# Tiles normalised and turned ahead of the seam: four in the token experts, six in cross attention with four tiles' gate logits

## The chip, the cores and the metric

One NeuronCore of a Trainium2 chip runs the whole kernel. Its engines are TensorE (matmuls and transposes into PSUM), VectorE, ScalarE, GpSimd and SyncE, which here only issues DMAs; each works through a queue of its own, and they wait for one another by semaphores. The metric is the time of one execution in microseconds (us), as the median of several; less is better.

## The reference, cut to what matters

A decoder of two layers on 1024 tokens of width 256, everything in float32 at the edges. Every step reads a layer norm of the running `x` and adds to it:

```python
x = x + linear_attention(layernorm(x))     # L0: 16 heads, decaying sums
x = x + token_experts(layernorm(x), ids)   # L0: 4 experts chosen by token id
x = x + retrieval(layernorm(x))            # L0: 2025 products of keys, top 8 of 8 heads
x = x + block_attention(layernorm(x))      # L1
x = x + cross_attention(layernorm(x), ctx) # L1: 16 heads of 16, quantised
h = layernorm(x)                           # L1: router
scores = sigmoid(h @ gate_w.T)
_, topk_idx = top_k(scores + bias, 2)      # of 16 experts
x = x + shared(h) + routed(h, topk_idx, scores)
```

The layer norm is `(x - mean) / sqrt(var + eps)` per token, without gain or offset.

## The kernel before

`x` lies in SBUF as 8 tiles (`NT`) of 128 tokens by 256. `xT` is the normalised and transposed state, 2 chunks (`DC`) of 128 by 1024 tokens. Each stage is a `Block`: within it every engine has its own list of instructions, and the next block begins when all engines have come to the end of theirs. This document calls that point a seam.

The layer norm is spread over seam and engines. In the tail of a stage, VectorE adds the result of a tile to `x` and takes its statistics (`norm_statistics`, L90); behind the eighth tile it writes the variances to `ln.rstd` (L104) and GpSimd raises them to the power -0.5 (`norm_pool`, L118). Behind the seam, VectorE normalises eight tiles (`norm_vector`, L111), TensorE turns each with two transposes (`norm_tensor`, L135, two PSUM banks in turn) and ScalarE copies each to `xT` (`norm_scalar`, L143). TensorE spends the wait at the end of a stage on products of the identity whose result nobody reads (`keep_busy`, L124; four calls are eight instructions in the trace).

The order of the work is written out by hand. At the first seam (A) `token_experts` ends with a product per tile (L479) and `private_state` begins. Its up products (L572, 8 groups of 4 instructions) read only the first 512 tokens of `xT`, the tiles 0 to 3. TensorE waits for the keys (L609) and for all eight copies (L610) before them. ScalarE follows each group with a silu (L632), and behind the last ones with casts (L1444) which VectorE's `quantise_context` (L1447 to L1480) needs.

At the second seam (B) `attend`, the core of cross attention, ends. It runs 128 units (8 tiles of 16 heads): scores on TensorE (L1761), their maximum and a bias on VectorE (L1822, L1824), the exponential on ScalarE (L1811), a cast on GpSimd (L1748), a DMA transpose that SyncE issues (L1733), and eight units later the mix with the values on TensorE (L1771). For each tile there follows a finish: `normalise` (L1834), two transposes (L1780), `scale_values` (L1846), the projection (L1786, L1787), and `residual` (L1851) with the statistics. For the tiles 0 to 6 it is done inside the loop over the next tile's units, for tile 7 it is the tail. Then `route` normalises and turns eight tiles, makes the gate's logits (L1999, 32 instructions), their sigmoid (L2019), and VectorE's selection (from L2033 on): the picks (L2048), from which TensorE counts ranks (L2006, L2009), and the slots (to L2073). `mix_experts` follows, the expert stage.

## Time and profile before

| | |
|---|---|
| median of 3 runs | 977.1 us (976.2 to 977.96) |
| profiled execution | 974.31 us, of which the span from first to last instruction is 972.3 |
| busy share of the span | TensorE 79%, VectorE 75%, GpSimd 58%, ScalarE 58% |
| mean granted TensorE clock | 0.894 of full speed |
| seam A | at about 137 us of the span |
| cross attention's units | from about 636 to 836 us |
| seam B | at about 847 us |

In the traces below PE is TensorE's matmuls, PEld its weight loads, DVE VectorE, ACT ScalarE, POOL GpSimd, SPq SyncE's queue; `out<-in` are the names of the program, and `x8` says that eight instructions were merged into one line whose length is theirs together. In brackets stands how long the engine was idle before, and what ended the wait. The time of an execution lies some 2 us above its span.

### The profile page before, as it was taken

The page shows a single profiled execution, that of the slowest core. Times are in us where ns is not written, and L with a number is a line of the kernel's source. Part 1 is how long each engine was busy: PE and PEld are TensorE (multiplying, and loading weights), DVE is VectorE, ACT ScalarE, POOL GpSimd, SP SyncE. Part 2 cuts the span into 40 slices and gives each one's busy share as a digit, 9 for nine tenths or more (in the row PEclk, how much of TensorE's full clock was granted, in tenths as well). Part 3 has the DMA queues.
Part 4 walks back from the last instruction along what each step waited for, and adds up shares of the span by engine and source line. Part 5 has one row for each costly group of instructions (what it writes and reads, how often), then busy time and mean ns, then how long its engine had stood idle before and what let it go on. Part 6 is the DMA issues. An engine that isn't in the chain of part 4 may idle for free. (4 is left out here: it accounts for less than half of the span.)

```text
span 972.3 us, 14012 instructions
## 1 busy us (share of the span) xinstructions
PE 764.8 (79%) x4650; PEld 495.1 (51%) x4673; DVE 727.4 (75%) x1281; ACT 561.6 (58%) x1035; POOL 563.7 (58%) x440
## 2 busy tenths in 40 slices
PE   4999998868776777788879988766766767789991
PEld 2564663437665666666663466623333333356550
DVE  4766357688999999999942754679999999454564
ACT  2314114778678768777741454678888888224540
POOL 3115300799699998998931132258777776314642
PEclk9999999999999988978989989958777786799996
DMA  5002021000000000000006000969999999322224
GB/s 178 1 0 87 1 84 54 0 1 1 1 1 0 1 1 1 1 0 1 1 1 233 1 1 2 307 116 186 185 170 178 182 168 172 67 93 71 85 70 162
DMA packets 149525, 69.61 MB, mean 72 GB/s; under 512 B 139003, under 2 KB 144909, under 8 KB 148302
## 3 DMA queue, kind: packets, MB, share of 16 engines
q1 hardware_dynamic: 147150, 62.42, 29.3%
q0 software_dynamic: 2304, 6.29, 2.2%
q8 instruction: 38, 0.62, 0.3%
q14 instruction: 33, 0.27, 0.1%
HBM read 27.46 MB, written 7.68 MB: 36 GB/s over the span
## 5 line engine op out<-in xcount | busy, mean ns | idle before, releaser
L773 POOL TENSOR_TENSOR r_pairs<-r_side_exp 128x945 f32<-128x945 f32 x104 | 183.6, 1804 | 0.0
L902 ACT ACTIVATE r_w<-r_w,r_down 128x1024 f32<-128x1024 f32 (+1 forms) x119 | 134.8, 1136 | 63.7 <-DVE r_w L1004 53.0
L1811 ACT ACTIVATE c_probs<-c_scores,c_bias,c_q_scale 128x1024 int16<-128x1024 f32 x128 | 154.1, 1204 | 29.8 <-DVE c_bias L1824 20.9
L1748 POOL CAST kv_parts<-c_probs 128x1024 bf16<-128x1024 int16 x128 | 132.1, 1039 | 54.6 <-ACT c_probs L1811 53.3
L1822 DVE TENSOR_REDUCE c_neg_max<-c_scores 128x1 f32<-128x1024 f32 x128 | 155.5, 1215 | 6.1 <-PE c_scores L1761 5.9
L843 PE MATMUL r_head_sum<-ident,r_w 128*128 128x128 f32 x952 | 125.2, 291 | 36.4 <-ACT ctxT L913 21.8
L1761 PE MATMUL c_scores<-c_kT,c_placed 128*128 128x512 bf16 x233 | 98.6, 509 | 57.7 <-ACT c_probs L1811 54.3
L843 PEld LDWEIGHTS r_head_sum<-ident,r_w 128*128 128x128 f32 x952 | 116.2, 153 | 52.2 <-issue 34.3
L994 DVE SCALAR_TENSOR_TENSOR r_chosen<-r_pairs,r_kept,r_z 128x1024 f32<-128x1024 f32 (+1 forms) x84 | 103.5, 1272 | 4.5 <-ACT r_pairs L892 3.3
L1004 DVE TENSOR_TENSOR r_w<-r_pairs,r_chosen 128x1024 f32<-128x1024 f32 (+1 forms) x78 | 91.2, 1204 | 0.0
L803 PE MATMUL r_head_sum<-r_up,ctxT 128*128 128x256 f32 x224 | 61.3, 441 | 19.3 <-ACT ctxT L913 19.3
L1771 PEld LDWEIGHTS c_mixed<-c_v,c_pT 128*128 128x128 bf16 x1024 | 45.1, 103 | 46.8 <-issue 24.4
L803 PEld LDWEIGHTS r_head_sum<-r_up,ctxT 128*128 128x128 f32 x224 | 49.7, 225 | 29.5 <-ACT ctxT L913 20.8
L118 POOL TENSOR_TENSOR ln_rstd<-ln_rstd,ln_minus_half 128x8 f32<-128x8 f32 x6 | 9.9, 1650 | 88.2 <-DVE ln_rstd L104 86.3
L1761 PEld LDWEIGHTS c_scores<-c_kT,c_placed 128*128 128x128 bf16 x256 | 16.8, 105 | 81.4 <-ACT c_probs L1811 75.6
L892 ACT ACTIVATE r_pairs<-r_side_exp 128x45 f32<-128x45 f32 x208 | 56.3, 320 | 0.0
L1771 PE MATMUL c_mixed<-c_v,c_pT 128*128 128x32 bf16 x1024 | 45.5, 183 | 5.3 <-DMA c_pT<-kv_parts 5.1
L1091 POOL TENSOR_TENSOR b_p<-b_p,b_row_sum 128x1024 f32<-128x1024 f32 x8 | 15.2, 1896 | 58.7 <-DVE b_row_sum L1085 58.7
L755 POOL TENSOR_TENSOR r_w<-r_pairs,r_w 128x1001 f32<-128x1001 f32 x18 | 38.9, 2162 | 16.1 <-DVE r_w L994 16.1
L794 PE MATMUL r_z<-r_down,r_hT 128*128 128x512 f32 (+1 forms) x64 | 33.4, 647 | 12.6 <-DVE r_chosen L994 12.4
L773 POOL TENSOR_TENSOR r_late_pairs<-r_side_exp 128x945 f32<-128x945 f32 x24 | 42.7, 1803 | 0.0
L2132 POOL DMA_INDIRECT pick_rows<-e_made,e_to_row x24 | 23.8, 990 | 29.6 <-DVE e_made L2307 24.5
(354 smaller groups left out, 1607.0 us busy)
## 6 DMA issues: line engine op xcount, KB each, us to landing
en_w<-in_w SPq DMA_DIRECT2D x1, 2992.0 KB, 12.1
ew_w<-in_w SPq DMA_DIRECT2D x1, 2992.0 KB, 12.1
ew_w_near<-in_w_near SPq DMA_DIRECT2D x1, 2176.0 KB, 20.9
r_up<-in_up SPq DMA_DIRECT2D x1, 2048.0 KB, 9.6
c_pT<-kv_parts SPq DMA_TRANSPOSE x128, 3.3
token_rows<-e_xn SPq DMA_DIRECT2D x2, 1024.0 KB, 5.8
e_row<-pick_rows SPq DMA_DIRECT2D x8, 256.0 KB, 4.6
zero_rows<-b_zeros SPq DMA_DIRECT2D x1, 1360.0 KB, 14.9
```

What stands on the lines that cost most here:

```text
L773: nc.gpsimd.tensor_tensor(pair_slot(v)[:, BY_ACT * KEYS:].rearrange("p (a b) -> p a b", b=KEYS), a.broadcast_to([P, ROWS - BY_ACT, KEYS]), ...
L803: last = nc.tensor.matmul(to, wT[0:n, b, :], r.up[0:n, b, :], start=(b == 0), stop=(b == PB - 1))
L843: last = nc.tensor.matmul(head_sum[0:m, b // 4, (b % 4) * P:(b % 4 + 1) * P], w_slot(v)[:, b * P:b * P + m], ident[:, :], start=(h == 0 an ...
L892: last = nc.scalar.activation(pair_slot(v)[:, a * KEYS:(a + 1) * KEYS], side_exp[:, t % 2, HEADS_R + h, 0:KEYS], ACT.Copy, scale=side_exp[ ...
L902: nc.scalar.activation(w_slot(v)[:, 0:COLS[f]], w_slot(v)[:, 0:COLS[f]], ACT.Silu, scale=scale[:, t % 2, h:h + 1]).then_inc(silu_done, 1)
L994: nc.vector.scalar_tensor_tensor(to, products(v), kept[:, t % 2, h, TOP - 1:TOP], flat(z[:, :, :], f), ALU.is_ge, ALU.mult).then_inc(picke ...
L1004: nc.vector.tensor_tensor(w_slot(v)[:, 0:COLS[f]], products(v), flat(chosen[:, (v - pool_count(v)) % 2, :, :], f), ALU.mult).then_inc(weig ...
L1748: nc.gpsimd.tensor_copy(rounded[:, u % ROUNDED, :], probs[:, u % RING, :]).then_inc(rounded_ready, 1)
L1761: last = nc.tensor.matmul(scores[:, u % SCORED, n, :], placed[:, t % 2, h // 2, h % 2, :], s.kT[:, h // 2, n * HALF:(n + 1) * HALF], start ...
L1771: last = nc.tensor.matmul(mixed[:, 0, h * PAIR_C:(h + 1) * PAIR_C], pT[:, u % TURNED, n, :], s.v[:, n, h // 2 * PAIR_C:(h // 2 + 1) * PAIR ...
L1811: nc.scalar.activation(probs[:, u % RING, :], scores[:, u % SCORED, :, :].rearrange("p a b -> p (a b)"), ACT.Exp, bias=bias[:, t, h:h + 1] ...
L1822: chain.step(nc.vector.tensor_reduce(neg_max[:, t, h:h + 1], scores[:, u % SCORED, :, :].rearrange("p a b -> p (a b)"), AX.X, ALU.max, neg ...
```

## The change

Four things. (1) `norm_statistics` and `norm_pool` can do the norm in two parts, and the loops over tiles are split into functions for one tile. (2) In `token_experts` the tiles 0 to 3 are normalised (while the tiles 5 and 6 are being added), turned and copied before the seam; `private_state` normalises and turns the tiles 4 to 7, and TensorE does so behind the first group of up products, with the wait for the keys moved to the last group and a wait for the earlier loads put first, on SyncE too. (3) In `attend` the statistics of the tiles 0 to 5 are closed at tile 5 and raised to the power behind the cast of unit 117. VectorE normalises these six after the residual of tile 6, TensorE turns four of them between the last mixes and two behind the last projection, into banks of the scores, and makes four tiles' gate logits, two of them ahead of the last projection; ScalarE copies and takes their sigmoid. The gate is loaded at the start of `attend`. `route` does the rest: tiles 6 and 7, and the logits of the tiles 4 to 7. The normalised rows lie in `ctxT`, over which the expert stage writes, so VectorE waits there until they are stored. (4) The identity products go from 4 calls to 2 at the end of the token experts, from 4 to none at the end of `attend`, and from 4 to 2 ahead of the ranks.

The diff, cut to its core:

```diff
...
-def norm_statistics(nc, eng, sh, t):
+def norm_statistics(nc, eng, sh, t, first=NT):
...
     ln = sh.ln
     nc.vector.bn_stats(ln.stats[:, t, :], sh.x[:, t, :]).then_inc(ln.steps, 1)
-    if t >= 1:
+    if t >= 1 and t != first:
         nc.vector.bn_aggr(ln.mv[:, t - 1, :], ln.stats[:, t - 1, :]).then_inc(ln.steps, 1)
         ln.step_count += 1
     ln.step_count += 1
     eng.wait_ge(ln.steps, ln.step_count)
-    if t == NT - 1:
+    if t in (first - 1, NT - 1):
+        part = slice(0 if t == first - 1 else first, t + 1)
         nc.vector.bn_aggr(ln.mv[:, t, :], ln.stats[:, t, :]).then_inc(ln.steps, 1)
         ln.step_count += 1
         eng.wait_ge(ln.steps, ln.step_count)
-        nc.vector.tensor_scalar(ln.rstd[:, :], ln.mv[:, :, 1], LN_EPS, None, ALU.add).then_inc(ln.var_ready, 1)
+        nc.vector.tensor_scalar(ln.rstd[:, part], ln.mv[:, part, 1], LN_EPS, None, ALU.add).then_inc(ln.var_ready, 1)
 def norm_vector(nc, eng, ln, x, chain):
-    eng.wait_ge(ln.rstd_ready, ln.norms + 1)
-    for t in range(NT):
+    eng.wait_ge(ln.rstd_ready, ln.norms + 1 + ln.extra)
+    norm_rows(nc, ln, x, range(NT))
+def norm_rows(nc, ln, x, tiles):
+    for t in tiles:
         nc.vector.tensor_scalar(ln.xn[:, t, :], x[:, t, :], ln.mv[:, t, 0:1], ln.rstd[:, t:t + 1],
                                 ALU.subtract, ALU.mult).then_inc(ln.normed, 1)
...
-def norm_pool(nc, pool, ln, norm):
...
-    pool.wait_ge(ln.var_ready, norm + 1)
-    nc.gpsimd.tensor_tensor(ln.rstd[:, :], ln.rstd[:, :], ln.minus_half[:, :], ALU.pow).then_inc(ln.rstd_ready, 1)
+def norm_pool(nc, pool, ln, norm, part=slice(0, NT)):
+    pool.wait_ge(ln.var_ready, norm + 1 + ln.extra)
+    nc.gpsimd.tensor_tensor(ln.rstd[:, part], ln.rstd[:, part], ln.minus_half[:, part], ALU.pow).then_inc(ln.rstd_ready, 1)
...
-        pe.wait_ge(ln.normed, ln.tiles + t + 1)
-        if t >= 2:
-            pe.wait_ge(ln.copied, ln.tiles + t - 1)
-        for c in range(DC):
...
-        last.then_inc(ln.turned_ready, 1)
+        norm_turn(nc, pe, ln, ident, ln.turned, ln.tiles, t)
+def norm_turn(nc, pe, ln, ident, turned, tiles, t):
+    pe.wait_ge(ln.normed, tiles + t + 1)
+    if t >= 2:
+        pe.wait_ge(ln.copied, tiles + t - 1)
+    for c in range(DC):
+        last = nc.tensor.transpose(turned[:, t % 2, c * P:(c + 1) * P], ln.xn[:, t, c * P:(c + 1) * P], ident[:, :])
+    last.then_inc(ln.turned_ready, 1)
...
     for t in range(NT):
-        act.wait_ge(ln.turned_ready, ln.tiles + t + 1)
-        nc.scalar.copy(place(t), ln.turned[:, t % 2, 0:D].rearrange("p (c n) -> p c n", c=DC)).then_inc(ln.copied, 1)
+        norm_copy(nc, act, ln, place(t), ln.turned, ln.tiles, t)
+def norm_copy(nc, act, ln, to, turned, tiles, t):
+    act.wait_ge(ln.turned_ready, tiles + t + 1)
+    nc.scalar.copy(to, turned[:, t % 2, 0:D].rearrange("p (c n) -> p c n", c=DC)).then_inc(ln.copied, 1)
...
+        FIRST = NT // 2
+        tiles = (ln.norms + 1) * NT
...
-            norm_pool(nc, pool, ln, ln.norms + 1)
+            norm_pool(nc, pool, ln, ln.norms + 1, slice(0, FIRST))
+            norm_pool(nc, pool, ln, ln.norms + 2, slice(FIRST, NT))
...
                 last.then_inc(out_ready, 1)
-            keep_busy(nc, up[:, 0, :], ident, 4)
+            for t in range(FIRST):
+                norm_turn(nc, pe, ln, ident, ln.turned, tiles, t)
+            keep_busy(nc, up[:, 0, :], ident, 2)
...
                 nc.scalar.activation(hid[:, e, f, h * HALF:(h + 1) * HALF], up[:, i % 4, :], ACT.Silu).then_inc(silu_ready, 1)
+            for t in range(FIRST):
+                norm_copy(nc, act, ln, xT[:, :, t * P:(t + 1) * P], ln.turned, tiles, t)
...
-                norm_statistics(nc, dve, sh, t)
+                norm_statistics(nc, dve, sh, t, FIRST)
+                if t == FIRST + 1:
+                    dve.wait_ge(ln.rstd_ready, ln.norms + 2 + ln.extra)
+                if FIRST < t < NT - 1:
+                    norm_rows(nc, ln, x, range(2 * (t - FIRST) - 2, 2 * (t - FIRST)))
...
+        ln.extra += 1
+        FIRST = NT // 2
...
             sp.wait_ge(zeroed, 1)
+            sp.wait_ge(loaded, PRIVATE_LOADS)
...
-            norm_tensor(nc, pe, ln, ident)
-            pe.wait_ge(loaded, PRIVATE_LOADS + 32)
-            pe.wait_ge(ln.copied, ln.tiles + NT)
+            pe.wait_ge(loaded, PRIVATE_LOADS)
+            pe.wait_ge(ln.copied, ln.tiles + FIRST)
             for c in range(UC):
+                if c == 1:
+                    for t in range(FIRST, NT):
+                        norm_turn(nc, pe, ln, ident, ln.turned, ln.tiles, t)
                 if c == UC - 1:
+                    pe.wait_ge(loaded, PRIVATE_LOADS + 32)
...
-            norm_scalar(nc, act, ln, lambda t: xT[:, :, t * P:(t + 1) * P])
-            act.wait_ge(loaded, PRIVATE_LOADS + 32)
+            for t in range(FIRST, NT):
+                norm_copy(nc, act, ln, xT[:, :, t * P:(t + 1) * P], ln.turned, ln.tiles, t)
+            act.wait_ge(loaded, PRIVATE_LOADS)
             for c in range(UC):
                 act.wait_ge(pw.up_ready, c + 1)
...
-            norm_vector(nc, dve, ln, x, chain)
+            dve.wait_ge(ln.rstd_ready, ln.norms + 1 + ln.extra)
+            norm_rows(nc, ln, x, range(FIRST, NT))
             quantise_context(nc, dve, chain, sh.cw, sh.kv)
...
+SOON, GATED = 6, 4
...
+    x, xT, ident, ln, g = sh.x, sh.xT, sh.ident, sh.ln, sh.gate
...
-        o, oT = sh.xT[:, 0, 0:D], sh.xT[:, 1, 0:D].rearrange("p (c n) -> p c n", c=DC)
+        o, oT = xT[:, 0, N - D:], xT[:, 1, N - D:].rearrange("p (c n) -> p c n", c=DC)
...
+        ln.xn = g.xn
+        tiles = (ln.norms + 1) * NT
+        ln_turned, logits = scores[:, (UNITS_C - 3) % SCORED, :, :], scores[:, (UNITS_C - 2) % SCORED, 0, :]
+        NORM_AT = UNITS_C - HEADS_C + PLACE_AT + 1
...
+            load_gate(sp, g, i)
             for u in range(UNITS_C):
                 sp.wait_ge(rounded_ready, u + 1)
...
                 nc.gpsimd.tensor_copy(rounded[:, u % ROUNDED, :], probs[:, u % RING, :]).then_inc(rounded_ready, 1)
-            norm_pool(nc, pool, sh.ln, sh.ln.norms + 1)
+                if u == NORM_AT:
+                    norm_pool(nc, pool, ln, ln.norms + 1, slice(0, SOON))
+            norm_pool(nc, pool, ln, ln.norms + 2, slice(SOON, NT))
...
+                    if t == NT - 1 and h >= HEADS_C - 3:
+                        n = 2 * (h - (HEADS_C - 3))
+                        if n == 0:
+                            pe.wait_ge(exp_done, UNITS_C)
+                            pe.wait_ge(g.loaded, 32)
+                        if n < SOON - 2:
+                            norm_turn(nc, pe, ln, ident, ln_turned, tiles, n)
+                            norm_turn(nc, pe, ln, ident, ln_turned, tiles, n + 1)
             finish_a(NT - 1)
+            pe.wait_ge(ln.copied, tiles + 2)
+            gate_logits(nc, g, xT, logits, range(2))
             finish_b(NT - 1)
-            keep_busy(nc, scores[:, 0, 0, :], ident, 4)
+            norm_turn(nc, pe, ln, ident, ln_turned, tiles, SOON - 2)
+            norm_turn(nc, pe, ln, ident, ln_turned, tiles, SOON - 1)
+            gate_logits(nc, g, xT, logits, range(2, GATED)).then_inc(g.logits_ready, 1)
...
+            for t in range(SOON):
+                norm_copy(nc, act, ln, xT[:, :, t * P:(t + 1) * P], ln_turned, tiles, t)
+            act.wait_ge(g.logits_ready, 1)
+            gate_scores(nc, g, logits, 0, GATED).then_inc(g.score_ready, 1)
...
-                norm_statistics(nc, dve, sh, t)
+                norm_statistics(nc, dve, sh, t, SOON)
...
             residual(NT - 2)
+            dve.wait_ge(ln.rstd_ready, ln.norms + 2 + ln.extra)
+            norm_rows(nc, ln, x, range(SOON))
             normalise(NT - 1)
             scale_values(NT - 1)
             residual(NT - 1)
...
+def gate_buffers(nc, ctx, sh):
+    sb, ps, sem = scope(nc, ctx, "g_")
+    g = sh.gate = Buffers()
+    g.xn = sh.ctxT[:, :, :].rearrange("p c n -> p (c n)").rearrange("p (t d) -> p t d", d=D)
+    g.w, g.bias = sb("w", [P, DC, EXPERTS]), sb("bias", [P, EXPERTS])
+    g.score = sb("score", [P, NT, EXPERTS])
+    g.loaded, g.logits_ready, g.score_ready = sem("loaded"), sem("logits_ready"), sem("score_ready")
+def load_gate(sp, g, i):
+    sp.dma_start(g.w[:, :, :], i["gate"]).then_inc(g.loaded, 16)
+    sp.dma_start(g.bias[:, :], i["bias"].broadcast_to([P, EXPERTS])).then_inc(g.loaded, 16)
+def gate_logits(nc, g, xT, bank, tiles):
+    for t in tiles:
+        for c in range(DC):
+            last = nc.tensor.matmul(bank[:, t * EXPERTS:(t + 1) * EXPERTS], xT[:, c, t * P:(t + 1) * P],
+                                    g.w[:, c, :], start=(c == 0), stop=(c == DC - 1))
+    return last
+def gate_scores(nc, g, bank, lo, hi):
+    return nc.scalar.activation(g.score[:, lo:hi, :].rearrange("p t e -> p (t e)"), bank[:, lo * EXPERTS:hi * EXPERTS], ACT.Sigmoid)
...
-        gate, bias = sb("gate", [P, DC, EXPERTS]), sb("bias", [P, EXPERTS])
+        g = sh.gate
+        ln.xn = s.xn = g.xn
+        bias, score = g.bias, g.score
...
-            sp.dma_start(gate[:, :, :], i["gate"]).then_inc(loaded, 16)
-            sp.dma_start(bias[:, :], i["bias"].broadcast_to([P, EXPERTS])).then_inc(loaded, 16)
...
-            norm_tensor(nc, pe, ln, ident)
-            pe.wait_ge(loaded, 32)
+            gate_logits(nc, g, xT, logits[:, 0, :], range(GATED, SOON))
+            for t in range(SOON, NT):
+                norm_turn(nc, pe, ln, ident, ln.turned, ln.tiles, t)
             pe.wait_ge(ln.copied, ln.tiles + NT)
-            for t in range(NT):
-                for c in range(DC):
-                    last = nc.tensor.matmul(logits[:, 0, t * EXPERTS:(t + 1) * EXPERTS], xT[:, c, t * P:(t + 1) * P],
-                                            gate[:, c, :], start=(c == 0), stop=(c == DC - 1))
-            last.then_inc(logits_ready, 1)
-            keep_busy(nc, ln.turned[:, 0, :], ident, 4)
+            gate_logits(nc, g, xT, logits[:, 0, :], range(SOON, NT)).then_inc(g.logits_ready, 1)
+            keep_busy(nc, ln.turned[:, 0, :], ident, 2)
...
-            norm_scalar(nc, act, ln, lambda t: xT[:, :, t * P:(t + 1) * P])
-            act.wait_ge(logits_ready, 1)
-            nc.scalar.activation(score[:, :, :].rearrange("p t e -> p (t e)"), logits[:, 0, 0:NT * EXPERTS],
-                                 ACT.Sigmoid).then_inc(score_ready, 1)
+            for t in range(SOON, NT):
+                norm_copy(nc, act, ln, xT[:, :, t * P:(t + 1) * P], ln.turned, ln.tiles, t)
+            act.wait_ge(g.logits_ready, 2)
+            gate_scores(nc, g, logits[:, 0, :], GATED, NT).then_inc(g.score_ready, 1)
...
-            norm_vector(nc, dve, ln, x, chain)
+            dve.wait_ge(ln.rstd_ready, ln.norms + 2 + ln.extra)
+            norm_rows(nc, ln, x, range(SOON, NT))
...
-            dve.wait_ge(loaded, 32)
-            dve.wait_ge(score_ready, 1)
+            dve.wait_ge(g.loaded, 32)
+            dve.wait_ge(g.score_ready, 2)
...
             dve.wait_ge(ew.loaded, EW_LOADS)
+            dve.wait_ge(s.rows_stored, 16 * KEPT)
...
+        gate_buffers(nc, ctx, sh)
...
```

## Rows read from the trace of the kernel before

**Rows 1.** Timeline, seam A: start, length, engine, line, operation, [idle before <- what ended it].
```profile
133.61 3.60 PE L124 MATMUL m_up<-ident 128*128 128x512 f32 x8
...
135.35 1.64 POOL L118 TENSOR_TENSOR ln_rstd<-ln_rstd,ln_minus_half 128x8 f32<-128x8 f32 x1 [27.81 <-DVE ln_rstd L104]
...
137.51 3.06 DVE L111 TENSOR_SCALAR r_ln_xn<-x,ln_mv,ln_rstd 128x256 f32<-128x256 f32 x8 [2.25 <-PEq L432]
```

**Rows 2.** The same timeline behind seam A, the private state.
```profile
138.37 0.76 PE L135 MATMUL r_ln_turned<-ident,r_ln_xn 128*128 128x128 f32 x4 [1.16 <-DVE r_ln_xn L111]
...
141.29 0.73 PE L135 MATMUL r_ln_turned<-ident,r_ln_xn 128*128 128x128 f32 x4 [0.23 <-ACT xT L143]
...
142.57 12.26 PE L572 MATMUL r_up<-xT,r_late_pairs 128*128 128x512 f32 x28 [0.55 <-ACT xT L143]
...
158.95 1.03 ACT L1444 CAST kv_parts<-cw_k 128x1024 bf16<-128x1024 f32 x1
...
169.33 1.23 DVE L1480 TENSOR_SCALAR kv_vTb<-cw_vT 128x2048 bf16<-128x2048 f32 x1
```

**Rows 3.** The timeline of cross attention's tail.
```profile
835.96 0.40 PE L1771 MATMUL c_mixed<-c_v,c_pT 128*128 128x32 bf16 x8 [1.60 <-DMA c_pT<-kv_parts]
836.45 0.49 DVE L1834 TENSOR_TENSOR xT<-c_mixed,c_row_sum 128x128 f32<-128x128 f32 x2 [4.46 <-PE c_mixed L1771]
...
837.00 0.69 PE L1780 MATMUL c_tail<-ident,xT 128*128 128x128 f32 x2 [0.64 <-DVE xT L1834]
...
838.39 2.08 PE L1786 MATMUL c_tail<-c_w_p,xT 128*128 128x256 f32 x4 [0.70 <-DVE xT L1846]
...
841.54 5.43 PE L124 MATMUL c_scores<-ident 128*128 128x512 f32 x8
841.65 0.42 DVE L1851 TENSOR_TENSOR x<-x,c_tail 128x256 f32<-128x256 f32 x1 [3.32 <-PE c_tail L1787]
...
843.12 1.64 POOL L118 TENSOR_TENSOR ln_rstd<-ln_rstd,ln_minus_half 128x8 f32<-128x8 f32 x1 [10.41 <-DVE ln_rstd L104]
```

**Rows 4.** The timeline of the router, and of the experts' first activation.
```profile
847.28 3.03 DVE L111 TENSOR_SCALAR e_xn<-x,ln_mv,ln_rstd 128x256 f32<-128x256 f32 x8 [4.24 <-PEq L1682]
...
851.96 3.94 PE L1999 MATMUL e_logits<-e_gate,xT 128*128 128x16 f32 x32 [0.55 <-ACT xT L143]
...
855.08 0.82 PE L1999 MATMUL e_logits<-e_gate,xT 128*128 128x16 f32 x4
...
855.74 5.15 PE L124 MATMUL e_ln_turned<-ident 128*128 128x512 f32 x8
...
856.32 0.29 DVE L2033 TENSOR_TENSOR e_chosen<-e_score,e_bias 128x128 f32<-128x128 f32 x1 [5.68 <-ACT e_score L2019]
...
859.43 0.29 DVE L2048 CAST e_pickedb<-e_picked 128x256 bf16<-128x256 f32 x1
...
860.84 1.12 PE L2009 MATMUL e_rank<-e_pickedb,e_onesb 128*128 128x256 bf16 x16
...
869.03 1.28 ACT L2262 ACT_TABLE_LOAD   x1
870.32 0.53 ACT L2262 ACTIVATE e_gated<-e_hidden 128x176 f32<-128x176 f32 x2
```

**Rows 5.** Windows: length, PE, PEld, DVE, ACT, POOL busy, granted clock, DMA, GB/s.
```profile
137.50:142.40 4.90, 2.94 (x16) 1.60 (x16) 4.88 (x10) 2.74 (x8) 0.67 (x1) 1.00 0.52 115
...
855.40:858.60 3.20, 3.20 (x7) 1.65 (x7) 2.22 (x25) 0.28 (x1) 0.00 (x0) 0.50 0.66 220
...
880.00:890.00 10.00, 10.00 (x56) 7.08 (x55) 4.10 (x8) 5.51 (x14) 7.57 (x8) 1.00 0.37 105
```

**Rows 6.** Timelines of DVE, ACT, POOL in the loop, at tile 5's residual.
```profile
812.23 0.16 DVE L96 BATCH_NORM_AGGREGATE ln_mv<-ln_stats 128x2 f32<-128x6 f32 x1
...
813.94 1.20 ACT L1811 ACTIVATE c_probs<-c_scores,c_bias,c_q_scale 128x1024 int16<-128x1024 f32 x1 [1.08 <-DVE c_bias L1824]
...
816.67 1.04 POOL L1748 CAST kv_parts<-c_probs 128x1024 bf16<-128x1024 int16 x1 [0.34 <-ACT c_probs L1811]
```

23 lines of the change are left out of this document (9 added, 14 removed).

## The prediction

> **What bounds the kernel now.** I read the page first. No engine is busy throughout, and the chain that ended last covers only the last tenth, so an engine's total says little about what a change is worth. I then read the timeline at the two places that the change touches. Both are seams between stages: the next stage starts when the last engine has arrived, and then normalises eight tiles, turns them on TensorE and copies them before its own work starts.
>
> Seam A, token experts to the private state: TensorE's identity products end at 133.61 + 3.60 = 137.21, GpSimd's power at 136.99, and the first instruction behind the seam starts at 137.51 [rows 1]. The eight tiles then take until the last pair is turned (141.29) and copied, and only at 142.57 does TensorE start the up products, 28 instructions in 12.26 us or 0.43 each [rows 2]. The rest of the stage hangs on them: ScalarE's cast at 158.95 stands behind the last of them, VectorE's context chain hangs on the casts, and its end (169.33 + 1.23 = 170.56) is the end of the stage [rows 2].
>
> Seam B, cross attention to the router: the last mix waits for its DMA, ends at 836.36, VectorE has been idle for 4.46, and then comes a chain without slack: finish, projection, residual at 841.65, power from 843.12 to 844.76. Identity products on TensorE run until 846.97, so they, not the power, end the stage [rows 3]. The router starts at 847.28 and its first selection instruction at 856.32, 9.04 us later; between them lie eight tiles, the logits (3.94) and the sigmoid [rows 4]. TensorE's clock in these stretches is in [rows 5].
>
> **Part 1, seam A.** Four tiles move in front of it. Before the seam VectorE gets two normalisations (0.38 each, 3.06 / 8 [rows 1]) at each of the tiles 5 and 6, inside waits for TensorE: free. GpSimd's power for them lies there too. TensorE turns four tiles behind its last product, two pairs at 0.97 a pair ((141.29 - 138.37) / 3 [rows 2]), the second one 0.7 without the wait behind it, so 1.7, and loses four of eight identity instructions (4 x 0.45 = 1.8). So TensorE arrives 0.1 earlier, and GpSimd arrives within 0.2 of that even if half the columns save nothing: 0.1 gained. Behind the seam the first up product needs only tiles 0 to 3. TensorE starts it at once (137.5), takes 4 x 0.43 = 1.7, turns the tiles 4 to 7 (0.97 + 0.7 = 1.7), and starts the second product at 140.9 to 141.1, where it now starts at 142.57 + 1.71 = 144.28: 3.3 gained. The wait for the keys moves behind seven products and vanishes. VectorE's context chain starts 1.2 sooner (four tiles less at 0.33, the first one being slower), which stays ahead of the casts. SyncE's added wait is for loads issued a stage earlier, which the up products wait for today too; behind it in its queue are the keys (due at the eighth product) and the two tables (due in the next stage), so it costs nothing. **Sum 3.4**, between 3.0 (each pair at 1.0, no arrival gain) and 3.7.
>
> **Part 2a, inside the loop of cross attention.** At tile 5 VectorE gets an aggregation earlier and a short add: 0.2 each with the wait between. VectorE and ScalarE are both back to back there; after the residual ScalarE waits 1.08 for VectorE [rows 6]. So 0.4 comes out at the end in full: **-0.4**. On GpSimd the power (1.65) follows the cast of unit 117; behind it are the casts, behind them SyncE's DMA transposes and TensorE's mixes. The casts take 1.04 and wait 0.34 each [rows 6], so 1.3 of delay is made up in four units of the ten left, and mixes run eight units later: 0, at most 1.3. The gate loads are first in SyncE's queue, two short issues while the first unit is still being scored: 0.
>
> **Part 2b, the tail.** Six normalisations (6 x 0.38 = 2.3) fit in VectorE's idle 4.46. Four turned tiles fit between the last mixes (1.60 of DMA wait before the last alone [rows 3]); their copies meet an idle ScalarE. Not covered: the logits of two tiles, queued on TensorE ahead of the last projection. The projection waits for VectorE until 838.39 anyway. The logits cost 8 of 32 instructions: 3.94 / 4 = 1.0 at the upper clock level, twice that at most at the lower one. The last four instructions, partly behind the fall, took 0.82, with about 0.3 of latency in it: 0.15 to 0.2 apiece [rows 4]. I take 1.6. TensorE is at its lower level there (0.50 in the profile is 1.2 GHz, 1.00 is 2.4): eight identity products took 5.43 here, 3.60 at seam A [rows 1, 3]. The projection then starts at 838.1 + 1.6 = 839.7, 1.3 late; the power ends at 846.1. TensorE turns the tiles 4 and 5 (1.1) and makes two tiles' logits (1.6) until 845.5. ScalarE loads the sigmoid's table, 1.28 [rows 4], behind the copy of tile 5 (from 844.3) and ends at 845.9. So the stage ends at 846.1, where the identity products now end it at 846.97. **+0.9**, with the 0.4 of part 2a already in it, since the mix ends at 836.8 and the finish starts at 837.4 here. If six columns fewer shorten the power, ScalarE ends the stage, 0.2 sooner.
>
> The Trainium skill, "ScalarE: Activation LUTs", What ACT_TABLE_LOAD costs, states a drain of about 1380 ns beside the 1283 ns load. The trace disagrees: the load of the experts' first activation starts at 869.03, takes 1.28 and the activation follows at 870.32, with no second stretch [rows 4]. By the page my sum would be about 1.2 less; by the trace it is as it stands.
>
> **Part 2c, the router.** Behind the seam: two tiles' logits 1.6, turning two tiles 1.1 (VectorE's two normalisations at 0.8 lie under the logits), a copy 0.4, two tiles' logits 1.6, latencies 0.2, sigmoid 0.3: 5.2 against 9.04. **+3.8.** Ends: all logits at 2.0 give 2.9; all at the upper level (0.9, 0.5, 0.4, 0.9) give 5.7. The table is already loaded. Identity products before the ranks fall from eight to four instructions; at the lower level they take 3.4, as long as VectorE needs from its selection to the picks (856.32 to 859.72). Now the eight run 5.15 from 855.74, beyond the picks [rows 4]. The ranks may gain 0.6, or lose 0.2 if their 1.1 doubles: **+0.2**. VectorE's new wait for the stored rows has its whole expert loop behind it, but the store follows the last normalisation, which comes over 2 us sooner, and the wait comes after the selection, the picks and the ranks, over 10 us later: 0.
>
> **Sum:** 3.4 + 0.9 + 3.8 + 0.2 = 8.3. The profiled execution took 974.31 (972.3 of span and 2.0 around it), 2.8 below the median of 977.1, within the scatter of such executions. 974.31 - 8.3 = 966.0, and from the median **968.8**.
>
> **The clock, for and against.** At seam A the profile shows 1.00 throughout 4.9 us in which TensorE did little but turn tiles [rows 5]. The change leaves fewer identity products ahead and an up product at once behind, so I charge nothing. The Trainium skill, "TensorE: Matmul & The Clock Gate", Part 4, says that transposes do not count as work for the clock in the same way. By it the up products might run at half rate for a while, four of them at 0.85 for 0.43, and part 1 would be 1.7 rather than 3.4; the trace disagrees with that for seam A. At seam B the level had fallen while TensorE waited for transfers, and came back in the 5.43 us of identity products, which the change removes. It fell again after the logits and returned after the next identity products (0.50 from 855.4 to 858.6 [rows 5]). So I put the whole of parts 2b and 2c at the lower level.
>
> **Rivals.**
> (a) The four turned tiles keep the clock up in the tail. For: it stayed up at seam A. Against: at seam B there are still idle pieces of 1.6 and no long products. Then the logits cost 1.0, the way from projection to residual half of 3.26, the stage ends at 843.8 (3.2 gained), the router gains 5.7 and the ranks 0.6: 3.4 + 9.5 = 12.9, so 964.2. Chance 0.13.
> (b) The second half gives back what it saves: the casts are not caught up (1.3), the four pairs of logits cost 2.0 each (1.6), the ranks double (0.4 against my value). 8.3 - 3.3 = 5.0, 972.1. For: the wait of 1.60 for a transfer in the tail. Chance 0.11.
> (c) The clock falls behind seam A, after the turned tiles: four products at 0.85, 8.3 - 1.7 = 6.6, 970.5. Against: [rows 5]. The Trainium skill's page on TensorE, cited above, would have it so. Chance 0.04.
> (d) The table switch stalls ScalarE for a second piece as long as the load: the sigmoid then ends 1.1 behind the power, 969.9. Against: 869.03 to 870.32. The Trainium skill's page on ScalarE, cited above, would have it so. Chance 0.03.
> (e) It moves nothing, because the stages behind the seams wait for something else. Against: neither shows an engine waiting for a load. 977.1 give or take 1.5. Chance 0.03.
> (f) Slower: the level lost at 837 stays down into the expert stage, where TensorE is busy 10.00 us in 10 at 1.00 [rows 5]. Each 10 us of that work at half the clock costs 10. The 8.3 are gone once 8 us of it run so; 20 us of it would give 989. Against: identity products stand before and behind the ranks, ahead of that stage, and the level came back while such products ran, from 841.5 on and again from 855.7 on. Chance 0.03.
> My forecast, with its own range 966.5 to 971.0, has the other 0.63.
>
> **How the numbers follow.** The range of 8 in 10 goes from 964.8 (short of (a)) to 972.2 (with (b)). About 0.2% is what a measurement of this kernel can tell from no change, that is 975.1 to 979.1. Faster by more: 0.94 (forecast, (a) to (d)); within: 0.03; slower: 0.03.
>
> **What would show it.** In the profile after: the first up product directly behind seam A, and the second 3.4 to 3.6 behind the seam's first instruction; the private state 3.4 shorter from there to VectorE's last context instruction; no ACT_TABLE_LOAD in the router; the selection starting 5.2 behind the router's start (3.3 if (a) holds) with the granted clock at 0.50 there; the tail from the last mix to the router's start 9.6 rather than 10.9. It would be wrong if the power on GpSimd held up casts to the end of the loop, if the stage behind seam A turned out bound by VectorE's context chain, or if the granted clock read 0.50 beyond the ranks.

## The result, and the profile after

The changed kernel takes 964.32 us (median of 4, 964.08 to 965.02), the kernel before 976.73 on the same chip (median of 4, 976.2 to 977.96). The ratio is 0.9877, with an interval of 0.985 to 0.9903: 12.4 us faster. The forecast was 968.8 in a range of 964.8 to 972.2: the sign was right, the time lies 0.5 below the range, and the gain, put at 8.3, was half as large again. The profiled execution took 965.02, against 974.31 before: by this one pair the gain is 9.3. The other 3.1 are there because the profiled execution of the kernel before lay 2.4 under its median and that of the changed one 0.7 above its own.

Seam A in the timeline of the changed kernel (columns as in [rows 1]):

```profile
134.29 0.42 DVE L537 TENSOR_TENSOR x<-x,m_out 128x256 f32<-128x256 f32 x1 [1.72 <-PE m_out L498]
...
135.55 1.88 PE L130 MATMUL m_up<-ident 128*128 128x512 f32 x4
135.76 1.01 POOL L124 TENSOR_TENSOR ln_rstd<-ln_rstd,ln_minus_half 128x4 f32<-128x4 f32 x1 [12.74 <-DVE ln_rstd L105]
...
137.74 1.77 DVE L117 TENSOR_SCALAR r_ln_xn<-x,ln_mv,ln_rstd 128x256 f32<-128x256 f32 x4 [2.06 <-PEq L448]
...
137.88 1.95 PE L599 MATMUL r_up<-xT,r_late_pairs 128*128 128x512 f32 x4 [0.45 <-PEq L448]
...
141.13 10.47 PE L599 MATMUL r_up<-xT,r_late_pairs 128*128 128x512 f32 x24
...
166.11 1.23 DVE L1516 TENSOR_SCALAR kv_vTb<-cw_vT 128x2048 bf16<-128x2048 f32 x1
```

The residual of tile 7 in the kernel before:

```profile
133.88 0.42 DVE L514 TENSOR_TENSOR x<-x,m_out 128x256 f32<-128x256 f32 x1 [2.49 <-PE m_out L479]
```

From this residual to VectorE's first instruction behind the seam it is now 3.45 us, where it was 3.63 [rows 1]. The first group of up products runs at once, the second starts 3.39 behind that instruction of VectorE, and the end of VectorE's context chain (166.11 + 1.23 = 167.34) lies 29.60 behind it, where it was 33.05 [rows 1, 2].

The tail of cross attention and the router:

```profile
832.63 0.42 PE L1814 MATMUL c_mixed<-c_v,c_pT 128*128 128x32 bf16 x8
...
834.17 1.73 PE L2003 MATMUL c_scores<-g_w,xT 128*128 128x16 f32 x8
...
835.74 2.05 PE L1829 MATMUL c_tail<-c_w_p,xT 128*128 128x256 f32 x4
...
840.41 1.28 ACT L2010 ACT_TABLE_LOAD   x1
840.44 0.69 POOL L124 TENSOR_TENSOR ln_rstd<-ln_rstd,ln_minus_half 128x2 f32<-128x2 f32 x1 [11.43 <-DVE ln_rstd L105]
841.71 0.22 ACT L2010 ACTIVATE g_score<-c_scores 128x64 f32<-128x64 f32 x1
...
842.24 1.86 PE L2003 MATMUL e_logits<-g_w,xT 128*128 128x16 f32 x8 [0.73 <-PEq L1718]
...
845.49 1.89 PE L2003 MATMUL e_logits<-g_w,xT 128*128 128x16 f32 x8 [0.46 <-ACT xT L159]
...
847.22 3.76 PE L130 MATMUL e_ln_turned<-ident 128*128 128x512 f32 x4
...
847.75 0.29 DVE L2119 TENSOR_TENSOR e_chosen<-g_score,g_bias 128x128 f32<-128x128 f32 x1 [4.02 <-ACT g_score L2010]
...
850.86 0.29 DVE L2134 CAST e_pickedb<-e_picked 128x256 bf16<-128x256 f32 x1
...
851.47 1.82 PE L2094 MATMUL e_rank<-e_pickedb,e_onesb 128*128 128x256 bf16 x16
```

The last mix ends at 833.05. The router starts 9.17 later (10.9 before [rows 3, 4]), the selection 5.51 behind its start (9.04 before [rows 4]). ScalarE's sigmoid ends the stage, at 841.93.

The windows of the changed kernel (length, then PE, PEld, DVE, ACT and POOL busy, granted clock, DMA, GB/s):

```profile
137.70:142.70 5.00, 4.48 (x16) 2.42 (x17) 4.93 (x7) 1.89 (x5) 0.69 (x1) 1.00 0.53 114
...
167.60:172.00 4.40, 4.34 (x8) 2.53 (x9) 0.70 (x7) 0.76 (x1) 0.00 (x0) 0.50 0.00 0
830.00:842.20 12.20, 10.68 (x60) 8.40 (x60) 3.69 (x14) 3.74 (x8) 0.69 (x1) 0.50 0.18 34
842.20:847.70 5.50, 5.00 (x21) 4.63 (x22) 1.26 (x6) 0.97 (x3) 1.71 (x9) 0.50 0.70 229
...
853.30:857.00 3.70, 3.52 (x8) 1.26 (x8) 3.47 (x9) 0.00 (x0) 0.00 (x0) 1.00 0.00 0
```

Behind seam A the clock is 1.00, in tail and router 0.50 throughout. It is also 0.50 at 167.6 to 172, where the kernel before had 1.00.

### The profile page after: what moved, and what is told of

Same layout as the page of the kernel before. It is cut to its first block and busy times, and to the rows that moved or that the text cites. A ratio compares the mean times of both kernels' runs of the same rounds, so it can differ in the third digit from the quotient of the medians.

```text
span 963.2 us, 13983 instructions
## 1 busy us (share of the span) xinstructions
PE 758.9 (79%) x4634; PEld 494.7 (51%) x4657; DVE 727.7 (76%) x1283; ACT 562.2 (58%) x1036; POOL 564.1 (59%) x442
## 5 line engine op out<-in xcount | busy, mean ns | idle before, releaser
L124 POOL TENSOR_TENSOR ln_rstd<-ln_rstd,ln_minus_half 128x8 f32<-128x8 f32 (+3 forms) x8 | 10.7, 1332 | 88.0 <-DVE ln_rstd L105 86.1
```

## Experiments

For each run I measured three stretches in its trace, in us: from the end of the last mix to the router's first instruction (one of GpSimd's, 0.02 ahead of VectorE's), from there to the selection, and from the selection to the end of the last rank product. One trace is one execution. The old form of a stretch is that of the kernel before, the new form that of the changed one:

| profiled execution | mix to router | to selection | to ranks | sum |
|---|---|---|---|---|
| old: before (the one predicted from) | 10.90 | 9.06 | 5.64 | 25.60 |
| old: before_again | 11.74 | 11.79 | 6.40 | 29.93 |
| old: before_third | 12.09 | 11.46 | 6.75 | 30.30 |
| old: seam_a_alone | 10.59 | 9.74 | 6.84 | 27.17 |
| old: seam_a_filled_gap | 10.63 | 9.68 | 6.90 | 27.21 |
| new: changed | 9.17 | 5.53 | 5.54 | 20.24 |
| new: changed_again | 9.17 | 5.53 | 4.78 | 19.48 |
| new: changed_third | 9.17 | 5.53 | 4.78 | 19.48 |
| new: seam_b_alone | 9.17 | 5.53 | 4.78 | 19.48 |
| new: changed_gap_filled | 9.17 | 5.53 | 4.81 | 19.51 |
| old, no identity products at the end: before_no_identity_b | 8.74 | 13.19 | 6.05 | 27.98 |
| old, filled tail: before_held | 10.79 | 11.42 | 6.78 | 28.99 |
| new, with them: changed_identity_b | 14.02 | 3.48 | 4.81 | 22.31 |
| new, four calls ahead of the ranks: changed_identity_ranks | 9.17 | 5.53 | 6.02 | 20.72 |
| new, filled loop: changed_warm_loop | 9.17 | 5.52 | 4.78 | 19.47 |
| new, filled tail: changed_warm_tail | 6.41 | 5.45 | 5.42 | 17.28 |
| new, filled tail: changed_held_last | 6.41 | 3.48 | 4.79 | 14.68 |
| new, filled tail: changed_held | 8.24 | 5.53 | 4.78 | 18.55 |

The first five rows, the old form, have 25.6 to 30.3, mean 28.04; the next five, the new form, 19.5 to 20.2, mean 19.64.

**seam_a_alone, seam_b_alone.** Each half of the diff by itself: the lines of `token_experts` and `private_state`, or those from `attend` on, with the helpers.

> Part 1 alone (seam A as in the changed kernel, everything from cross attention on as before). Theory 1, the seams give what the trace after shows and the rest of the 12.4 us comes from the clock in no fixed place: 3.7 us faster than before (the end of VectorE's context chain moved by 3.70 us between the two traces, counted from the start of the stage before), that is 973.0. Theory 2, the unexplained 4 us belong to seam A, because the clock falls there in most executions of the kernel before and not in its profiled one: 7 to 8 us faster, about 969. Theory 3, they belong to the second half: 3.4 to 3.7, as theory 1, and the run of part 2 alone tells them apart.

> Part 2 alone (cross attention and router as in the changed kernel, seam A as before). Theory 1: 4.9 us faster (the shift between the traces from the last loop of cross attention, 3.70, to the experts, 8.64), that is 971.8. Theory 2 (surplus at seam A): 4.9 as well. Theory 3 (surplus in cross attention and the router): 8.5 to 9, about 968.

Measured: 0.9968 of before (0.9938 to 0.9998) for part 1 and 0.9908 (0.9878 to 0.9938) for part 2, so 3.1 and 9.0 us by the 976.73 of before. The whole was 0.9883 beside them, 11.4 us by the same 976.73: the parts add up within their intervals. Part 1 (0.2 to 6.1) is as forecast. Part 2 gives 9.0 (6.1 to 12.1) where the sum had 4.9: the surplus is there (theory 3).

**changed_again, before_again, before_third.** No edit.

> The changed kernel once more, unchanged, for a second profile and a paired time: 12.4 us faster again, 0.987 to 0.988 of before. Theory 1: the fall of the clock at 167 us, which took 2.97 us of the private state's gain in the first profile, is in another place or gone, and other falls have moved. If falls stand at fixed places of the kernel: it is there again.

> The kernel before once more, for a second profile. Theory 1: the two profiles of one kernel differ in the places where the clock falls, and between two falls the shift is constant; span 972 to 976. Theory 2: the second profile shows TensorE's clock at 0.50 somewhere in 133 to 145 us, with the up products at 0.85 apiece, and is 3 to 4 us longer there. If falls stand at fixed places: the two profiles agree within 0.3 us throughout.

> The kernel before a third time, as it is. If the first profiled execution was a favourable draw of the clock at seam B, its 25.6 us from the last mix to the end of the ranks stay the smallest: 27 to 30 here (29.9, 27.2 and 27.2 in three other traces with that stretch unchanged). If 25.6 is the usual value, the surplus of the measured gain over the predicted one has another place.

changed_again: 0.9883 (0.9846 to 0.9921). before_again and before_third are single executions, of 989.00 and 978.50 us on chips where the kernel before has medians of 990.16 and 975.32. The fall at 167 us is a matter of the execution: in the first profile of the changed kernel the r_chosen products took 8.04, in changed_again the stretch from the context chain's end to theirs was 5.41 instead of 8.37. The fall had moved to 203 us. The first rows below are of before, the second of changed:

```profile
170.88 5.08 PE L826 MATMUL r_chosen<-r_to_sims,r_hT 128*128 128x360 f32 x16 [2.99 <-PEq L579]
```

```profile
167.66 8.04 PE L861 MATMUL r_chosen<-r_to_sims,r_hT 128*128 128x360 f32 x16 [2.99 <-PEq L606]
```

The first two profiles of before agree within 1.3 us up to 800 us. By the last mix they lie 2.5 apart, as the first one's loop has a wait of 1.33 more, and at seam B they part (the 987.2 of span of before_again come from a slower expert stage as well, see the last section). before_third, seam B:

```profile
841.30 6.62 PE L124 MATMUL c_scores<-ident 128*128 128x512 f32 x8
...
842.88 1.64 POOL L118 TENSOR_TENSOR ln_rstd<-ln_rstd,ln_minus_half 128x8 f32<-128x8 f32 x1 [10.27 <-DVE ln_rstd L104]
...
848.23 3.20 DVE L111 TENSOR_SCALAR e_xn<-x,ln_mv,ln_rstd 128x256 f32<-128x256 f32 x8 [5.43 <-PEq L1682]
...
853.12 6.13 PE L1999 MATMUL e_logits<-e_gate,xT 128*128 128x16 f32 x32 [0.55 <-ACT xT L143]
...
859.09 6.25 PE L124 MATMUL e_ln_turned<-ident 128*128 128x512 f32 x8
...
859.67 0.29 DVE L2033 TENSOR_TENSOR e_chosen<-e_score,e_bias 128x128 f32<-128x128 f32 x1 [7.91 <-ACT e_score L2019]
```

```profile
841.30:848.20 6.90, 6.63 (x9) 2.52 (x8) 1.28 (x5) 0.00 (x0) 1.64 (x1) 0.57 0.00 0
...
852.50:859.00 6.50, 5.95 (x33) 5.92 (x32) 0.00 (x0) 1.75 (x3) 0.00 (x0) 0.62 0.96 318
859.00:863.00 4.00, 4.00 (x7) 1.92 (x7) 3.16 (x30) 0.28 (x1) 0.00 (x0) 0.50 0.01 2
```

Set beside [rows 3, 4]: the same eight identity instructions 6.62 instead of 5.43, so the stage ends behind them (847.92), 3.4 after the power (844.52); the logits 6.13 instead of 3.94; the next eight 6.25 instead of 5.15. GpSimd's power is 1.64 in both. VectorE's normalisations have grown by 0.17; the rest that has grown runs on TensorE, in windows whose granted clock is 0.57, 0.62 and 0.50. The execution on which the prediction rests was the cheapest of five in this stretch.

**before_no_identity_b.**

```diff
-            keep_busy(nc, scores[:, 0, 0, :], ident, 4)
```

> The kernel before without the eight identity instructions at the end of cross attention, nothing else. Theory (they set the end of the stage and bring the clock back): the stage ends 0.3 behind GpSimd's power, 8.7 us behind the last mix instead of 10.9 to 11.7, and the router runs at the lower level throughout, so that its selection comes 12 us behind its start instead of 9.06. From the last mix to the end of the ranks 26 us: no gain from taking them out alone. Rival, the level comes back by the router's own turned tiles: 9 to 10 us, sum 23 to 24. Second use: seam A in its old form once more, 23.3, 23.3 and 25.9 us so far.

As the theory had it, with the router a little dearer: 8.74, then 13.19 at the lower level, 27.98 in all, and 975.19 us for the execution. In the old form the identity products about broke even (mean 28.04 with them), as far as one execution can tell: 1.9 to 3.4 us later at the seam, 1.4 to 4.1 sooner at the selection.

**changed_identity_b.** The four calls back, behind the changed kernel's last logits.

```diff
             gate_logits(nc, g, xT, logits, range(2, GATED)).then_inc(g.logits_ready, 1)
+            keep_busy(nc, scores[:, 1, 0, :], ident, 4)
```

> The changed kernel with the eight identity instructions back at the end of cross attention. Theory: the router starts 13.9 us behind the last mix instead of 9.17 (5.4 us of identity products behind the logits, less what ScalarE needed there, 0.7), and as the level is back, its selection comes 3.3 us behind the start instead of 5.53; from the last mix to the end of the ranks 22 instead of 19.5 to 20.2, the whole 2 to 2.5 us slower than the changed kernel, so 9.5 us faster than before. Rival, the level isn't back by then: 5.5, and 4.5 us slower than the changed kernel.

```profile
843.05 5.45 PE L130 MATMUL c_scores<-ident 128*128 128x512 f32 x8
848.79 1.04 PE L2004 MATMUL e_logits<-g_w,xT 128*128 128x16 f32 x8 [0.30 <-PEq L1718]
...
850.83 1.06 PE L2004 MATMUL e_logits<-g_w,xT 128*128 128x16 f32 x8 [0.52 <-ACT xT L159]
```

14.02 and 3.48, within 0.2 of the forecast, and 22.31 in all, within 0.3 of it. The level is back and eight logits instructions take 1.04 to 1.06 instead of 1.86. The time was 0.9894 of before (0.9833 to 0.9956). In the new form only 2.05 us of the router are left for the upper level to save, and the products cost 4.85: by the trace, taking them out is right there. The times alone (0.9894 here, 0.9877 without) don't tell the two apart.

**changed_identity_ranks.**

```diff
-            keep_busy(nc, ln.turned[:, 0, :], ident, 2)
+            keep_busy(nc, ln.turned[:, 0, :], ident, 4)
```

> The changed kernel with four calls of identity products ahead of the ranks as before, instead of two. Theory: at the lower level, which held there in every trace of the changed kernel, eight instructions take 6.3 to 7 us and reach beyond the picks, which VectorE has 3.4 behind the selection: the stretch from the selection to the end of the ranks is 6.4 to 6.9 us, as in three of four traces of the kernel before, where the changed one has 4.78. The fewer identity products are then worth 1.6 to 2.1 and not the 0.2 of the prediction. Rival, nothing: 4.8 to 5.5.

```profile
842.14 5.48 PE L130 MATMUL e_ln_turned<-ident 128*128 128x512 f32 x8
847.45 0.27 PE L2091 MATMUL e_rank<-e_pickedb,e_earlier 128*128 128x256 bf16 x1
```

6.02 instead of 4.78: the eight instructions end at 847.62, and the ranks queue behind them. It is less than forecast since the level rose within them (5.48 rather than 6.3 to 7). So the two calls less are worth 0.5 to 1.2 by this one execution, not 0.2. It took 960.76 us, where the kernel before has 975.32; a single time says nothing on a difference of this size.

**seam_a_filled_gap, changed_gap_filled.** Six instructions where TensorE had nothing to do; the second also without `keep_busy` in `token_experts`.

```diff
             last.then_inc(pw.low_ready, 1)
+            keep_busy(nc, up[:, 0, :], ident, 3)
```

> Part 1 alone, with six identity instructions more at the end of the private state, where TensorE has nothing to do for 2.99 us (164.66 to 167.66 in the changed kernel's trace). Theory: the fall of the clock that makes the sixteen r_chosen products take 8.04 instead of 5.08 us follows that idle stretch and depends on where in time it comes to lie. Then the stretch from the end of VectorE's context chain to the end of r_chosen is 5.4 us here and would be so in every execution, the context chain ends as before, and the time is 3 to 6 us under the kernel before (part 1 alone was 3.2 under it). Rival, the fall comes from the turned tiles or the fewer identity products at seam A: 8.4 us again. Second use: a third look at seam B in its old form, whose stretch from the last mix to the end of the ranks was 25.6, 29.9 and 27.2 us so far.

> The changed kernel with two edits at seam A: no identity products there at all (two calls less), and three calls (six instructions) at the end of the private state. From the traces: TensorE's identity products end at 137.43 and GpSimd's power at 136.77 in the changed kernel, so the private state starts 0.6 us sooner; the stretch from the end of the context chain to the end of r_chosen is 5.40 in every draw, where the changed kernel had 8.37, 5.41 and 6.79. Together 0.6 and on average 1.5, so about 2 us under the changed kernel, 0.9855 to 0.986 of before. If the identity products at seam A were what holds the level there, the up products behind the seam read 0.85 apiece instead of 0.43 and the stretch from the seam to the low products is 2 to 4 us longer than 19.87.

```profile
164.50 2.74 PE L130 MATMUL r_up<-ident 128*128 128x512 f32 x6
167.65 5.08 PE L862 MATMUL r_chosen<-r_to_sims,r_hT 128*128 128x360 f32 x16 [0.41 <-PEq L606]
```

In seam_a_filled_gap r_chosen takes 5.08 and the stretch 5.40, as expected, though the kernel as a whole was not told apart from part 1 alone (0.996, 0.993 to 0.9991). But before_no_identity_b, with seam A in its old form, showed the 8.3 as well, so this fall is no price of the change. In changed_gap_filled the private state started 0.6 sooner, as TensorE and not GpSimd had been last, and the up products ran at the upper level without any identity product ahead. The stretch was 6.78, though: there the clock had fallen at 157, behind another idle piece (2.46 us), the products ahead took 8.59 instead of 7.10, and my six instructions then came out last. The time was 0.9873 (0.9839 to 0.9908): no difference from the changed kernel.

**changed_warm_loop, changed_warm_tail.**

```diff
+                    if 2 <= h < HEADS_C - 1:
+                        width = min(P, (HEADS_C - 1 - h) * PAIR_C)
+                        nc.tensor.matmul(mixed[:, 0, HALF - width:], ident[:, :], ident[:, 0:width], start=True, stop=True)
...
+                    if t == NT - 1 and HEADS_C - MIX_LAG < h < HEADS_C - 3:
+                        pe.wait_ge(exp_done, UNITS_C)
+                        keep_busy(nc, scores[:, 1, 0, :], ident, 1)
```

> The changed kernel with one identity product (up to 128 columns, two instructions) behind the mix in 13 of 16 units of cross attention's loop, in columns that later mixes write over. It asks what rival (a) would be worth. If the level stays up through the tail and the router: 7.1 to 7.4 us from the last mix to the router instead of 9.17, 3.3 to 3.5 to the selection instead of 5.53, ranks 0.6 sooner; and the loop, 190.7 to 193.5 us so far with the level down in more than half of it, is shorter too, by up to 8 us, since projections and scores run in half the time. Together 5 us or more under the changed kernel. If the added products don't hold the level: the loop 0 to 3 us longer (two instructions of 0.2 us per unit on an engine that is ahead of the chain) and the rest as in the changed kernel.

> The kernel with the added product per unit, and with four calls of 512 columns more between the last tile's mixes (heads 9 to 12), where TensorE waits for transfers. It asks again what rival (a) is worth. If that keeps the level up from 827 on: 7.1 to 7.4 us from the last mix to the router instead of 9.17, 3.3 to 3.5 to the selection instead of 5.5. If the level falls all the same, behind the turned tiles and the logits: 9.17 and 5.5 as in all three traces, and the last mix comes up to 1 us later, because the added instructions take 0.9 apiece.

The product in the loop (first three lines) raised the clock there (0.88 from 700 to 760 us, instead of 0.80 in the changed kernel's first trace and 0.70 in changed_again) and moved the loop by nothing that shows (191.33 us; 190.7 to 193.5 in the other traces): the loop isn't bound by TensorE. At 827 the level fell all the same, and the tail was 9.17. With the tail filled too it held: 6.41. But the fillings cost as much ahead: 7.49 from the last exponential to the last mix instead of 5.23. Times 0.9856 (0.9806 to 0.9907) and 0.988 (0.9837 to 0.9923).

**before_held, changed_held, changed_held_last, changed_third.** In changed_held the product in the loop stops at head 8 of the last tile, and with it come the two edits of changed_gap_filled and these; changed_held_last has the product in the last tile alone; before_held has it in the loop, and the calls for heads 10 to 14.

```diff
+                    if t == NT - 1 and 10 <= h < 13:
+                        pe.wait_ge(exp_done, UNITS_C)
+                        keep_busy(nc, scores[:, 1, 0, :], ident, 1)
...
             gate_logits(nc, g, xT, logits, range(2, GATED)).then_inc(g.logits_ready, 1)
+            keep_busy(nc, scores[:, 1, 0, :], ident, 1)
```

> The kernel before with one identity product (up to 128 columns) behind the mix in most units of the loop and five calls of 512 columns between the last tile's mixes, so that TensorE isn't idle ahead of seam B. If the scatter of the old form is the clock's: granted clock 1.00 from 830 us to the router's logits, identity products at the end of the stage 3.6 us instead of 5.1 to 6.3, and 7.4 us from the last mix to the router instead of 10.6 to 12.1; the router 8.6 to 9.1 to the selection, the rest below 6. Sum about 22 instead of 25.6 to 30.3. If the stretch hangs on something else: 10.6 or more.

> The changed kernel with the two edits of changed_gap_filled, the product per unit in the loop, three calls of 512 columns between the last tile's mixes (heads 10 to 12) and one behind the last logits of cross attention. If the level stays up: 6.4 us from the last mix to the router (as changed_warm_tail measured), 3.5 to the selection instead of 5.5, 4.8 for the ranks, so 14.7 instead of 19.5, at a cost of 0.3 to 1 us ahead of the last mix. Together 4 us under the changed kernel, 0.983 to 0.984 of before. If the added instructions hold up the mixes as in changed_warm_tail (7.49 from the last exponential to the last mix instead of 4.8 to 5.5): 2 us under it. If the level falls at 827 all the same: nothing gained, 0 to 1 us lost.

> The same without the product per unit in the tiles 0 to 6. If the level at the tail depends only on what TensorE does in the last tile: as changed_held. If the level that the loop hands over counts, the tail runs at the lower level in some draws: 9.17 and 5.5 and up to 2.5 us more ahead of the last mix, since the added instructions then take twice as long.

> The changed kernel as it is, for a paired time on the same chip: 0.987 to 0.988 of before, and from the last mix to the end of the ranks 19.5 to 20.2 once more.

changed_held_last, timeline and window:

```profile
832.39 0.96 PE L2010 MATMUL c_scores<-g_w,xT 128*128 128x16 f32 x8
...
833.26 1.13 PE L1829 MATMUL c_tail<-c_w_p,xT 128*128 128x256 f32 x4
...
837.91 1.04 PE L2010 MATMUL e_logits<-g_w,xT 128*128 128x16 f32 x8 [0.55 <-PEq L1718]
...
831.50:837.90 6.40, 5.24 (x30) 3.72 (x31) 2.38 (x9) 2.28 (x5) 0.70 (x2) 1.00 0.00 0
```

Here the level stays at 1.00 through the whole tail. Logits 0.96 instead of 1.73, projection 1.13 instead of 2.05, 6.41 to the router, 3.48 to the selection, 14.68 in all, and 5.89 ahead of the last mix, 0.7 more than in the changed kernel. In changed_held's profiled execution, at 984.54 us the slowest of its six, the level fell at 843 and the stretches were 8.24, 5.53 and 4.78. The times: 0.9821 of before (0.9778 to 0.9865) for changed_held, 0.9862 (0.9821 to 0.9904) for changed_held_last, 0.9896 (0.9855 to 0.9937) for changed_third, medians 973.01, 977.61 and 979.65 on a chip where before took 991.23. changed_held has the lowest ratio of this study, some 6 us under the changed kernel; the intervals overlap by 0.1%, so that is likely rather than shown, and no trace shows one of its faster executions.

before_held missed: the level was down from about 831 to 835 and fell again at 842, ahead of the identity products at the end, which took 6.66, and the sum was 28.99 (a single execution, 996.25 us). The old form was not held up, so the proof that its scatter is the clock's alone rests on before_third's rows, not on this run.

## Why the prediction was wrong, point by point

**The two traces agree with the sum.** The sum was made against the profiled execution: 8.3. The two profiled executions differ by 9.3, and they differ in luck elsewhere too. By stretches: arrival at seam A 0.18 (forecast 0.1); from there to the end of the context chain 3.45 (3.3); from the last mix to the router 1.73 (1.3, of 0.9 and the loop's 0.4); router to selection 3.53 (3.8); selection to ranks 0.10 (0.2). Against it the loop's two instructions, put at 0.4, cost 0.29: ScalarE's wait behind tile 5's residual is 1.37 instead of 1.08 [rows 6]. And 0.38 came that I had put at nothing: the last mix ends 5.23 behind the last exponential instead of 4.85. Together 8.3.

```profile
810.24 1.21 ACT L1866 ACTIVATE c_probs<-c_scores,c_bias,c_q_scale 128x1024 int16<-128x1024 f32 x1 [1.37 <-DVE c_bias L1883]
813.98 1.33 POOL L124 TENSOR_TENSOR ln_rstd<-ln_rstd,ln_minus_half 128x6 f32<-128x6 f32 x1
815.25 3.01 POOL L1789 CAST kv_parts<-c_probs 128x1024 bf16<-128x1024 int16 x3
819.17 1.04 POOL L1789 CAST kv_parts<-c_probs 128x1024 bf16<-128x1024 int16 x1 [0.91 <-ACT c_probs L1866]
```

The 0.38 are not the turned tiles' doing. The last mix starts 0.05 behind the landing of its own transfer, as it did before; it is the transfer that comes later. Part 2a had GpSimd's delay made up in four units, and on GpSimd it was: the power for six tiles (1.33), three casts back to back, and a wait of 0.91 already before the next. Behind GpSimd stands SyncE's queue, though, and there it was not. The last cast and the issue of the last transpose, first in the kernel before, then in the changed one:

```profile
831.66 1.04 POOL L1748 CAST kv_parts<-c_probs 128x1024 bf16<-128x1024 int16 x1 [0.85 <-ACT c_probs L1811]
832.73 1.23 SPq L1733 DMA_TRANSPOSE c_pT<-kv_parts  x1
```

```profile
827.97 1.04 POOL L1789 CAST kv_parts<-c_probs 128x1024 bf16<-128x1024 int16 x1 [0.86 <-ACT c_probs L1866]
829.51 1.30 SPq L1774 DMA_TRANSPOSE c_pT<-kv_parts  x1
```

The issue starts 0.03 behind the cast before, 0.50 behind it now. A unit comes every 1.38 us and most issues take 1.23 to 1.30, so a delay in this queue hardly shrinks: behind the power it was 1.0 for the units 121 to 126. How much of it is left is a matter of the execution. In seven traces with this tail unchanged the last issue starts 0.03 to 0.73 behind its cast, and the mix ends 4.8 to 4.9 behind the exponential in four of them and 5.2 to 5.5 in three; the old form has 4.7 to 4.85 in five. In these three the issue for unit 119, the second one behind the power, took 2.05 to 2.30, in the other four 1.28. One such long issue, 1.47 to 2.20 for unit 120, stands in the five traces of the old form too, and the change didn't bring it; that it and GpSimd's delay add up in the queue fits the rows, but no run tested it.

**The step that failed** is the last: "2.8 below the median of 977.1, within the scatter of such executions". I carried the gain from one execution over to the median as if the 2.8 lay where the change doesn't reach. By the traces most of them lay where it does. The mean of the five old executions has 28.04 us from the last mix to the ranks, the profiled one 25.60, so 2.4 less; the new form has 19.64 on average. So the terms were mis-sized for the median, the router's (3.8) and the ranks' (0.2) most of all:

- mix to router: 11.19 - 9.17 = 2.0 on average (1.73 in the pair), less 0.37 ahead of the last mix and 0.29 in the loop: 1.4 (forecast 0.9);
- router: 10.35 - 5.53 = 4.8 (3.8);
- ranks: 6.51 - 4.94 = 1.6 (0.2). Eight identity instructions at the lower level reach beyond the picks. In the profiled execution half of them ran at the upper one. changed_identity_ranks gives 0.5 to 1.2 of it to the two calls less; the rest is not assigned;
- seam A: 23.3 us from GpSimd's first instruction behind the seam to the down products in five of six old executions, 25.9 in seam_b_alone, where the clock fell at 143; 19.87 in all nine of the new form with its identity products. On average 3.9, with the arrival 4.1 (3.4).

Together 11.9, against 12.4 measured; the first three are 7.8, against 9.0 (6.1 to 12.1) for part 2 alone. These means are of five or six traces, so they carry some tenths of a microsecond of chance, at seam B about one. The changed form is not only shorter but has little left that scatters at seam B: 9.17 and 5.53 in five executions of five. In the first of them the level is the lower one throughout (830.00 to 847.70 at 0.50).

**The rivals.** (a) would have given 964.2, almost the measured time, and did not happen: its sign was a clock above 0.50 in the tail, and the clock read 0.50. A time that fits is no evidence for the mechanism that foretold it. What (a) is worth where it is made to happen: 6.41 + 3.48 instead of 9.17 + 5.53, 4.8 us, against the 4.2 that I had put on it (3.2 - 0.9 and 5.7 - 3.8). (b) came in a small part, 0.4 at the last mix by way of SyncE's queue; the logits of two tiles cost 1.73 to 1.89, not 2.0, and the ranks doubled (1.82 instead of 1.12) in the first of the five traces alone, which is why they gained only 0.10 there. (c) is refuted: four up products behind the turned tiles take 1.95, at 1.00. By the Trainium skill's "TensorE: Matmul & The Clock Gate", Part 4, by which transposes do not count as work for the clock in the same way, the level might have fallen there; in this stretch the trace disagrees. Without the four identity instructions ahead it fell in one of three executions (changed_held, at 140: 21.57 instead of 19.87), so these four may earn their 0.6. (d) is refuted: the table load starts at 840.41, takes 1.28, and the sigmoid starts at 841.71, with no second stretch. The Trainium skill's "ScalarE: Activation LUTs", What ACT_TABLE_LOAD costs, states a drain of about 1380 ns beside it; the measurement decides. (e) is refuted by the ratio. (f) is refuted by the ratio too: the level rose at 853, behind the ranks' identity products, and the window from 853.3 to 857 read 1.00.

Two ends of part 2c were added up wrongly by 0.1: with all logits at 2.0 the router gains 3.0, not 2.9, and with all at the upper level 5.8, not 5.7. Nothing hangs on it.

What stays open: whether the clock alone makes the old form's scatter (the rows of before_third point to it, the run meant to force it failed), what sets the place of the falls, and why a single issue at SyncE now and then takes up to 2.3 us.
